# GNN kernel: a buffer and a count for each late attribute tile, loaded at halves 3 and 10 in place of 7 and 13

## The reference

```
h = relu(layernorm(x));  x = x + attention_network(h, W, a, edge_weight, src, dst)
h = relu(layernorm(x));  x = x + three_layers(h):
for i in range(3):
    msg = relu(h[src] + edge_attr)                 # 200000 x 128
    aggr = segment_sum(msg, dst, 6250)
    t = relu(batchnorm((h + aggr) @ W1[i] + b1[i]))
    h = batchnorm(t @ W2[i] + b2[i])               # relu after it, except in the last layer
```

## Time and profile before

| what | value |
|---|---|
| median of 3 runs | 4149.84 us |
| lowest, highest | 4148.54, 4171.91 us |
| span of the profiled execution | 4143.2 us |
| PE busy | 3880.3 us (94%) |
| DVE busy | 3557.9 us (86%) |
| ACT busy | 3079.1 us (74%) |
| POOL busy | 2863.9 us (69%) |
| first late load to last late scatter | 1891.87 to 2553.7 us |

### The profile page before, as it was taken

The page is one execution under the profiler, slowest core; times in us unless marked ns, Lnnn a source line. Parts: engine busy times, 40 slices in busy tenths (PEclk is TensorE's granted clock), DMA queues, the critical chain, the costliest instruction groups (busy, mean ns, idle before and its releaser), DMA issues.

```text
span 4143.2 us, 151501 instructions
## 1 busy us (share of the span) xinstructions
PE 3880.3 (94%) x50473; PEld 3749.5 (90%) x50475; DVE 3557.9 (86%) x6826; ACT 3079.1 (74%) x7853; POOL 2863.9 (69%) x2594
## 2 busy tenths in 40 slices
PE   3899996899999999979999999899999989999998
PEld 3899996899999999969999999689999968999996
DVE  7799984677777777778888888789999988999997
ACT  4799994677777777767677667678888867888886
POOL 0288883777777777766777777367777736777773
PEclk7888898999999999989999999999999999999999
DMA  9988789898889898868999999689999958999995
GB/s 138 218 274 279 251 280 342 229 249 247 249 248 249 247 252 249 253 208 290 311 322 312 315 311 326 206 268 316 315 319 314 319 189 266 316 314 317 313 323 186
DMA packets 710002, 1132.45 MB, mean 273 GB/s; under 512 B 157402, under 2 KB 535084, under 8 KB 709564
## 3 DMA queue, kind: packets, MB, share of 16 engines
q1 hardware_dynamic: 493068, 787.26, 57.2%
q10 hardware_dynamic: 133200, 176.14, 17.3%
q0 software_dynamic: 83552, 166.66, 12.8%
HBM read 883.83 MB, written 246.33 MB: 273 GB/s over the span
## 4 chain that ended last, share of the span: by engine, by line
PE 66%; POOL 13%; DMA 6%; issue 6%; SPq 5%; DVE 3%; ACT 2%; DVEq 0%; POOLq 0%; ACTq 0%; PEld 0%; PEldq 0%
PE ps L2015 17%; PE ps L1938 14%; PE ps L2035 12%; PE ps L1925 11%; POOL attr_by_slot L874 9%; PE ps L2059 6%; POOL unit_x L938 4%; DMA unit_x<-gin_rows,unit_src 2%; PE ps L2038 2%; PE ps L2106 2%; DMA src_row<-rows_by_group 1%; DMA attr_by_slot<-late_attr,late_ridx 1%; PE ps L2049 1%; DMA abuf<-in_edge_attr 1%; SPq L663 1%
## 5 line engine op out<-in xcount | busy, mean ns | idle before, releaser
L938 POOL DMA_INDIRECT unit_x<-gin_rows,unit_src x1449 | 1457.8, 1006 | 500.2 <-issue 336.3
L874 POOL DMA_INDIRECT attr_by_slot<-abuf,ridx x1020 | 1279.6, 1255 | 486.0 <-issue 310.0
L2015 PE MATMUL ps<-x_parts,src_turned 128*128 128x128 bf16 x15876 | 1138.4, 222 | 26.2 <-ACT ps L1155 22.8
L2015 PEld LDWEIGHTS ps<-x_parts,src_turned 128*128 128x128 fp8e4 x15876 | 949.4, 99 | 71.8 <-issue 29.4
L1155 ACT ACTIVATE ps<-sums 128x512 f32<-128x512 f32 x1512 | 825.8, 546 | 187.2 <-DVE all_split_msg L1677 69.1
L1062 ACT ACTIVATE val<-ps,val 128x128 f32<-128x128 f32 x2597 | 717.9, 375 | 182.7 <-DVE val L1514 182.7
L1670 DVE TENSOR_TENSOR dst_hot<-ps,dl_slot 128x896 fp32r<-128x896 f32 x756 | 816.5, 1080 | 0.2
L1938 PE MATMUL ps<-val,src_hot 128*128 128x129 f32 x5194 | 693.0, 283 | 0.9 <-DVE sums L1454 0.3
L2035 PE MATMUL ps<-all_split_msg,dst_hot 128*128 128x256 f32 x3528 | 649.5, 304 | 10.5 <-DVE all_split_msg L1677 10.5
L1163 ACT ACTIVATE all_split_msg<-ps 128x512 fp32r<-128x512 f32 x1008 | 543.8, 539 | 148.9 <-PE ps L2015 121.1
L1677 DVE SCALAR_TENSOR_TENSOR all_split_msg<-ps,all_split_msg 128x512 fp32r<-128x512 f32 x1008 | 607.7, 615 | 15.8 <-ACT all_split_msg L1163 12.6
(11 more groups left out here) (266 smaller groups left out, 5752.5 us busy)
## 6 DMA issues: line engine op xcount, KB each, us to landing
sums<-attr_by_slot SPq DMA_DIRECT2D x756, 448.0 KB
turned_hot<-rows_by_block ACTq DMA_DIRECT2D x392, 384.0 KB
attr_by_slot<-zeros SPq DMA_DIRECT2D x36, 3136.0 KB
unit_attr<-in_edge_attr SPq DMA_DIRECT2D x204, 448.0 KB
abuf<-in_edge_attr SPq DMA_DIRECT2D x68, 960.0 KB
src_turned<-src_hots SPq DMA_DIRECT2D x504, 112.0 KB
src_row<-rows_by_group SPq DMA_DIRECT2D x252, 112.0 KB
src_hots<-src_turned SPq DMA_DIRECT2D x252, 112.0 KB
```

The lines of the kernel that those rows point to most:

```text
L874: pool.indirect_dma_start(out=attr_table, out_offset=bass.IndirectOffsetOnAxis(ap=ridx[:, g, t0 + t:t0 + t + 1], axis=0), in_=abuf[:, k % ...
L938: pool.indirect_dma_start(out=unit_x[:, half_place(k), t, :], out_offset=None, in_=gin_rows[n], in_offset=bass.IndirectOffsetOnAxis(ap=uni ...
L2015: ins = pe.matmul(ps[:, BANK[h], k * D:(k + 1) * D], src_turned[:, b * P:(b + 1) * P], x_parts[:, part, b, :], start=False, stop=(k == til ...
```

## The change

`late_attr` becomes a buffer of two tiles, one for each late group. Tile `r` has its own counts: it is loaded on `s_abuf[r]` and scattered on `s_scat[r]`, where `abuf`'s two buffers left them at the same value. The load of tile `r` with group `i` waits for the scatter of tile `r` with group `i - 1`. In SP's order the late loads stand at halves 3 and 10 in place of 7 and 13. Ahead of groups 34 and 35 SP waits on both counts. The scatters keep their places in POOL's order.

```
-LATE_LOAD_AT = (7, 13)
+LATE_LOAD_AT = (3, 10)
...
-        late_attr, at = placed("late_attr", [P, 1, D], F32, at)
+        late_attr, at = placed("late_attr", [P, len(LATE_GROUPS), D], F32, at)
...
-        def late_tile(i, r):
-
-            return 2 * (i - LATE_FROM) + r
...
             def load_late(i, r):
-                q, g = late_tile(i, r), LATE_GROUPS[r]
-                sp.wait_ge(s_scat[0], 16 * (SCATTERED + q))
+                g = LATE_GROUPS[r]
+                sp.wait_ge(s_scat[r], 16 * (SCATTERED + i - LATE_FROM))
                 of = edge_attr[g * GE:(g + 1) * GE].rearrange("(p t) d -> p t d", t=T)
-                sp.dma_start(late_attr[:, :, :], of[:, bass.ds(i - LATE_FROM, 1), :]).then_inc(s_abuf[0], 16)
+                sp.dma_start(late_attr[:, r:r + 1, :], of[:, bass.ds(i - LATE_FROM, 1), :]).then_inc(s_abuf[r], 16)
...
-                    sp.wait_ge(s_scat[0], 16 * (SCATTERED + 2 * T))
+                    for r in range(len(LATE_GROUPS)):
+                        sp.wait_ge(s_scat[r], 16 * (SCATTERED + T))
                     for i in LATE_GROUPS:
                         load_group(n, i)
...
             def scatter_late(i, r):
-                q = late_tile(i, r)
-                pool.wait_ge(s_abuf[0], 16 * (LOADED + q + 1))
+                pool.wait_ge(s_abuf[r], 16 * (LOADED + i - LATE_FROM + 1))
                 pool.indirect_dma_start(
                     out=attr_table, out_offset=bass.IndirectOffsetOnAxis(ap=late_ridx[:, r, i - LATE_FROM:i - LATE_FROM + 1], axis=0),
-                    in_=late_attr[:, 0, :], in_offset=None).then_inc(s_scat[0], 16)
+                    in_=late_attr[:, r, :], in_offset=None).then_inc(s_scat[r], 16)
```

## The result

The changed kernel takes 4108.35 us (median of 4 runs, 4106.91 to 4109.36); the kernel before, with one more run beside these, 4153.77 us. The ratio is 0.9899, 95% interval 0.9879 to 0.9919. The profiled execution has a span of 4106.9 us, 36.3 less than before. So the sign was right and the size wrong: by the ratio 42 us less (the medians lie 45.4 us apart) where 10 were forecast, outside the range.

What follows compares the result with a forecast made beforehand. POOL, 97% full in layer 1's late groups, was taken as the bound; 6.8 us of late-load waits and 3 us of PE waits would go, about -10 us, from 4149.84 to 4140 us, range 4121 to 4155.

Steps and rivals of the forecast that it cites:

- The bound: Late groups of layer 1: POOL 97% full, no group faster than 21.43 us whatever SP does, against a 21.90 us period.
- the cycle: Late tiles through one buffer: 6.2 us scatter start to next load, 5.6 us load to scatter, 23.6 us for two tiles.
- What POOL gets back: POOL's idle time beyond 0.30 us an instruction in the late stretch: -10 us, bounds 0 and -20.
- Late loads: POOL's wait for late loads: all 6.8 us go, each load having 11 us to its scatter against 5.6.
- PE: POOL's waits for PE: 3 of 4.0 us go, as PE is less late without ACT's stalls.
- Waits without releaser: POOL's waits with no releaser: 9.1 us in the late stretch, left in place as unrelated to this buffer.
- What a gather costs: Late-stretch gathers on POOL, lengthened by DVE's adds: mean stays 1.042 us; at 1.000 it would give 17 us more.
- SP and ACT: SP keeps 1 to 3 us wait at half 3; ACT's 60.7 us mostly go, but DVE's gather waits replace them.
- The two edits: Two buffers with two counts, and loads at halves 3 and 10: buffer cycle 11.8 us, no longer a limit; issue costs nothing.
- Rival B: POOL gets faster too, adds shifting off gathers: -27 us, 4123 us, chance 0.15; full 43 us (4107) 0.03 of it.
- D: Slower: SP's new rhythm starts every DVE add together with a gather, +12 us, 4162 us, chance 0.09.
- signs of being right: SP's late-scatter wait under 80 us, POOL's late-load wait 0, ACT's under 20, DVE's above 50.5, period 21.3 to 21.7, gather 1.03 to 1.05.

Runs made afterwards that it cites:

- add_5_12: Changed kernel with DVE's add of a unit one half later in all layers (5 and 12, not 4 and 11); ratio 1.0086 to the kernel before, layer 1 748.2 us.
- b_blocked: Changed kernel, loads at halves 3 and 10, with the kernel before's SP waits put back at halves 7 and 13; ratio 0.9915, layer 1 729.7 us.

## Why the prediction was wrong

**The bound.** This is the step that failed: POOL's 21.43 us taken as a floor that the change leaves standing, so that only 10 us of POOL's idle time could come back. I worked out both numbers: two tiles through one buffer at 23.6 us by the two measured legs, POOL at 21.43 us, period 21.90. I called them "about equally tight" and then let POOL alone set the floor, because it was 97% full and waited only 9.2 us for late loads. That share was a poor witness. Its line held 45.8 us by which gathers and scatters ran longer than undisturbed ones, and 20.8 of these went with the change. With POOL made light the cycle kept 35 of the 37 us, so a lighter POOL alone would not have brought the gain. The 23.6 us were too many all the same: the load leg of 5.6 us came from a tile that POOL had waited for, and over the 60 tiles it is 5.10 us with POOL's turn in it, and with 6.02 us for the other leg that is 22.2 us for two.

**What POOL gets back (-10 us).** The same failure, term by term. Late loads: 6.8 us forecast and 6.8 found. PE: 3 forecast, 2.4 found. Waits without releaser: I left 9.1 us in place, "nothing to do with this buffer as far as the rows tell"; 7.1 of them went. Nearly all of this is four gaps of 0.9 to 3.4 us, some 145 us apart, where the changed kernel has none above 0.5. The one buffer alone doesn't make them, since the run without late tiles has three of 4.7 to 4.9 us in layer 1. What they are is not shown. And the durations: I held the mean gather at 1.042 us, a term of 0, and 20.8 us of busy time went. The four make the 37.1 us of POOL's line.

**What a gather costs.** The row that I read was right, the rule drawn from it not. A gather that starts inside an add of DVE is longer (up to 1.84 us in the kernel before), and in add_5_12 POOL spent 25 us more at adds. But I put all 42 us of lengthening on the adds, 0.71 us each; 21.3 belong to them, and 20.7 to the turns of the source rows, which I had not looked at. That the other stretches have shorter gathers because the add "finds no fixed place there" was wrong too: in layer 2 of the kernel before, gathers that overlap an add are 23.1 us too long together, as much as in the late groups, and those that overlap none take 0.945 us against 0.997. Layer 2 has no such turns. And I argued that a POOL-bound order fixes the add on a gather. The changed kernel has POOL fuller and the lengthening at adds a third as large (6.4 us against 21.3): fewer gathers start inside an add, 36 against 47, and 16 of the 36 start in its last 0.1 us, where there is nothing left to wait for. The Trainium skill (SBUF — State Buffer, section Who interferes with whom) says that whoever is first keeps the ports. By that rule a gather which starts just before the add loses nothing, and the trace agrees. It doesn't show the other side of the rule, an add that waits for the gather: the 59 adds of the late groups that start inside an instruction of POOL take 1.07 to 1.09 us, and those of the kernel before that start clear of one take no less. In the changed kernel two adds stand just behind the start of their gather, and these gathers are not long, while a gather that starts inside the first add is:

```profile
2181.29 1.08 DVE L1696 TENSOR_TENSOR unit_attr<-unit_attr,unit_x 128x896 f32<-128x896 f32 x1
...
2181.80 1.39 POOL L934 DMA_INDIRECT unit_x<-gin_rows,unit_src  x1 [0.30 <-issue]
...
2190.24 0.94 POOL L934 DMA_INDIRECT unit_x<-gin_rows,unit_src  x1 [0.30 <-issue]
2190.70 1.09 DVE L1696 TENSOR_TENSOR unit_attr<-unit_attr,unit_x 128x896 f32<-128x896 f32 x1 [0.16 <-DMA unit_x<-gin_rows,unit_src]
...
2201.86 0.96 POOL L934 DMA_INDIRECT unit_x<-gin_rows,unit_src  x1 [0.30 <-issue]
2201.92 1.07 DVE L1696 TENSOR_TENSOR unit_attr<-unit_attr,unit_x 128x896 f32<-128x896 f32 x1
```

**The lead.** I took POOL's 21.43 us as the period from the first late group on. POOL starts with a lead, and with 20.8 us a group against PE's 20.4 that lead lasts some 20 groups: the periods of the first 19 are 20.3 to 20.6 us, only the last eleven are 20.6 to 21.9. The run with a lead of 7 halves is 11.3 us longer, which fits, though its layers without late tiles grew too.

**SP and ACT.** Right in direction: ACT's 60.7 us of waits went, SP's 156.3 too. I expected a remainder of 1 to 3 us at half 3 and there is none. That DVE's wait for gathers would grow in their place was wrong, by the same step. Right too was that SP's block is not itself the loss (6 us by b_blocked).

**The two edits.** I costed them together. The second buffer with its count is all of it that can be told (724.7 us with the old halves); the halves alone give 4 us.

**The rivals.** Rival B had the right parts, lead apart: gathers back to 1.000 and more. I gave its full form 3 in 100 because it needed 0.98 us an instruction with POOL setting the pace; in fact 473 instructions at 0.998 us were enough, since the lead made up the rest. D's mechanism, gathers lengthened by adds, exists, but the change moved it the other way. add_5_12 has it together with a late message, so its +0.9% is no measure of D alone. Of the signs of being wrong that I had named, "a period near 20.5 (POOL was not the bound, or gathers shortened)" is the one that came. Three of the signs of being right came with it (SP's wait, POOL's for late loads, ACT's for chunk loads), so these three could not tell the rivals apart.

## What to carry to other kernels

When a load and the consumer that frees its buffer form a ring, add up the legs of the ring and compare them with the period before looking at who waits: a busy in-order queue in the ring can hide nearly all of the waiting (9 us shown, 35 us at stake), and leaving out some of its other work is the quick way to see it. Don't take durations from inside a disturbed stretch as the floor without it; the same instructions in a quiet stretch of the same profile (1.000 us a gather) came nearer to what was found (0.993) than the disturbed ones (1.042). And before a per-group deficit is multiplied by the number of groups, take off what a lead hides.

## What the runs showed of the hardware

A gather's issue on POOL takes 0.94 to 0.97 us when it meets neither an add nor a turn of DVE. When a gather starts within a 1.09 us add of two SBUF operands it ends 0.81 to 0.92 us after that add (46 of 47 in the kernel before), so it takes up to 1.84 us; behind a 0.68 us turn of the source rows it is 0.81 to 0.85 us (up to 1.41 us for the gather). A turn that starts 0.24 to 0.46 us into a gather makes it end 0.12 us after the turn, so it takes 1.03 to 1.26 us. An add that starts during a gather did nothing to it: the 52 in the late groups of the two kernels that no turn meets take 0.94 or 0.95 us. One half's shift of the add in a loop of 14 halves made the kernel 0.9% slower than before, where with the adds in their place it is 1.1% faster; how much of this is the gathers is not shown. In the kernel before, with the DMA engines busy for over 90%, a scatter's start on POOL and the release of SP were 6.0 us apart in the mean (5.1 to 6.8), and a load of 64 KB landed 3.9 us after its issue in the median (1.9 to 6.5). And chips differ: the kernel before took 5105 us on one of them and 4136 to 4154 us in every other comparison.
